# Attention with relative positions on one core: six heads of sixteen by a product over all distances instead of four, softmax sums by columns of ones, an update on GpSimd

## The reference, cut to what matters

```
x = _layernorm(src, ln1_g, ln1_b)
q, k, v = (x @ wq), (x @ wk), (x @ wv)            # 16 heads of 8
pos = arange(S - 1, -S, -1)                       # all distances
p = (concat([sin(pos * w), cos(pos * w)]) @ wp)   # (2S - 1, 16, 8)
ac = einsum('bihd,bjhd->bhij', q, k)
bd_full = einsum('bihd,phd->bhip', q, p)
bd = bd_full[:, :, i, i - j + S - 1]              # shift by the row
att = softmax((ac + bd) * scale, axis=-1)
src = src + einsum('bhij,bjhd->bihd', att, v) @ wo
x2 = _layernorm(src, ln2_g, ln2_b)
sel = sigmoid(x2 @ sel_w); scores, idx = top_k(sel, 4)
...                                               # experts, src + moe_out
x = x + 0.5 * L1_ffn(layernorm(x))
```

## Time and profile before

| | |
|---|---|
| median of 3 runs | 2732.15 us |
| the profiled execution's own time | 2728.11 us |
| its span, first to last instruction | 2726.4 us |
| PE busy, share of the span | 2436.3 us, 89% |
| DVE busy | 1929.8 us, 71% |
| ACT busy | 1581.3 us, 58% |
| POOL busy | 1557.1 us, 57% |
| mean granted clock of PE | 0.963 |

### The profile page before, as it was taken

The page is one execution under the profiler, slowest core; times in us unless marked ns, Lnnn a source line. Parts: engine busy times, 40 slices in busy tenths (PEclk is TensorE's granted clock), DMA queues, the critical chain, the costliest instruction groups (busy, mean ns, idle before and its releaser), DMA issues. The chain is left out here.

```text
span 2726.4 us, 59982 instructions
## 1 busy us (share of the span) xinstructions
PE 2436.3 (89%) x19038; PEld 1835.0 (67%) x19038; DVE 1929.8 (71%) x5169; ACT 1581.3 (58%) x4641; POOL 1557.1 (57%) x2343
## 2 busy tenths in 40 slices
PE   7999799799977999999988988999799999998898
PEld 5788677578865777777777335665577777777733
DVE  4554388455546899999876456776589999987645
ACT  2332244333326999999930226777699999993022
POOL 4322666332324678888743655554567888874365
PEclk9999899899998999999999997999899999999999
DMA  3720366370005455555455126553445545445512
GB/s 121 311 82 1 74 141 141 120 301 1 1 22 137 124 137 140 137 136 137 130 186 151 46 62 143 114 111 82 105 130 136 137 135 142 137 127 178 158 53 64
DMA packets 302396, 326.64 MB, mean 120 GB/s; under 512 B 31718, under 2 KB 274150, under 8 KB 294902
## 3 DMA queue, kind: packets, MB, share of 16 engines
q1 hardware_dynamic: 252934, 280.83, 37.9%
q0 software_dynamic: 12288, 25.19, 3.3%
q10 hardware_dynamic: 36864, 16.79, 2.1%
HBM read 133.36 MB, written 185.01 MB: 117 GB/s over the span
## 5 line engine op out<-in xcount | busy, mean ns | idle before, releaser
L2073 DVE TENSOR_REDUCE a_nm<-a_sr 128x2 f32<-128x512 f32 x256 | 166.9, 685 | 69.2 <-PE a_sr L1805 68.2
L3207 POOL TENSOR_TENSOR f4o_kv<-a5b_room 128x256 f32<-128x256 f32 x192 | 140.2, 731 | 107.7 <-DVE a5b_room L3075 102.6
L3207 POOL TENSOR_TENSOR f6o_kv<-a5b_room 128x256 f32<-128x256 f32 x192 | 140.3, 731 | 97.6 <-DVE a5b_room L3075 91.8
L2978 ACT ACTIVATE f6a_pr<-f6a_sr,f6a_nm 128x256 f32<-128x256 f32 x384 | 181.4, 486 | 12.0 <-DVE f6a_nm L3063 10.9
L2978 ACT ACTIVATE f4a_pr<-f4a_sr,f4a_nm 128x256 f32<-128x256 f32 x384 | 181.4, 486 | 9.5 <-DVE f4a_nm L3063 7.8
L3075 DVE TENSOR_TENSOR a5b_room<-f4a_ur,f4a_turn 128x512 f32<-128x512 f32 x192 | 131.2, 684 | 44.1 <-PE f4a_ur L2815 43.7
L2837 PE MATMUL f6a_sr<-all_ks,all_qs 96*128 96x256 bf16 x512 | 144.0, 281 | 13.6 <-ACT f6a_pr L2978 10.1
L2837 PE MATMUL f4a_sr<-all_ks,all_qs 96*128 96x256 bf16 x512 | 143.7, 281 | 13.8 <-ACT f4a_pr L2978 10.4
L3075 DVE TENSOR_TENSOR a5b_room<-f6a_ur,f6l_turn 128x512 f32<-128x512 f32 x192 | 131.5, 685 | 34.4 <-PE f6a_ur L2815 33.9
L2854 PE MATMUL f6a_tr<-all_table,f6a_pr 128*128 128x128 f32 x1024 | 154.8, 274 | 0.0
L2854 PE MATMUL f4a_tr<-all_table,f4a_pr 128*128 128x128 f32 x1024 | 154.7, 273 | 0.0
(11 more groups left out here) (672 smaller groups left out, 8481.8 us busy)
## 6 DMA issues: line engine op xcount, KB each, us to landing
slots<-f_zero SPq DMA_DIRECT2D x100, 512.0 KB, 6.1
f4a_slide<-f4o_kv SPq DMA_DIRECT2D x64, 383.0 KB
f6a_slide<-f6o_kv SPq DMA_DIRECT2D x64, 383.0 KB
f4o_kv<-f4a_slide SPq DMA_DIRECT2D x64, 256.0 KB
f6o_kv<-f6a_slide SPq DMA_DIRECT2D x64, 256.0 KB
f4o_src<-slots SPq DMA_DIRECT2D x128, 64.0 KB, 2.2
slots<-f4m_y ACTq DMA_DIRECT2D x128, 64.0 KB, 2.3
f6o_src<-slots SPq DMA_DIRECT2D x128, 64.0 KB, 2.2
```

The lines of the kernel that those rows point to most:

```text
L2073: nc.vector.tensor_reduce(nm[:, r // 2, t, at_:at_ + 2], sr[:, g % SB, :].rearrange("p (x s) -> p x s", x=2), AX.X, ALU.max, negate=True). ...
L2978: last = nc.scalar.activation(pr[:, n % 4, x, :], from_, ACT.Exp, bias=nm[:, n % SB, x:x + 1], scale=sign, accum_out=zs[:, b[1], t, h:h + 1])
L3207: nc.gpsimd.tensor_tensor(rr[:, o % RAW, :], tmp[:, o % 2, 0, :], tmp[:, o % 2, 1, :], ALU.add)\
```

## The change

Six parts, all in the attention of f4 and f6, and none elsewhere:

1. Heads 1, 3, 5, 9, 11 and 13 slide, instead of 1, 5, 9, 13. The table of distances in SBUF now holds heads that are not evenly spaced, so it is filled by 18 DMAs instead of 3 (once, in f4).
2. The softmax sums no longer come from ACT's accumulator. The value matrix gets columns of ones beside each pair of heads, set once, so that the product with the values also gives the sums; `y` uses 512 columns of its bank instead of 256.
3. At the end of a batch ACT copies `y` (512 columns), PE transposes it (four blocks), DVE takes reciprocals of the sums and multiplies, PE transposes back (two blocks), ACT copies, then `wo` follows.
4. x gets its half of the result by two POOL instructions in slot 15 instead of one DVE instruction in slot 9.
5. The small work stands in other slots.
6. SP's order has six shifts in a step: 9, 11, 13, then 1, 3, the write, then 5.

```
-SLID = H // QUAD
+SLIDING = (1, 3, 5, 9, 11, 13)
+SLID = len(SLIDING)
...
-            rows = bass.AP(part.tensor, part.offset + QUAD * OFFSETS, [[P * OFFSETS, run], [H * OFFSETS, HD], [1, SLID * OFFSETS]])
-            sp.dma_start(self.ms[first * HD:(first + run) * HD, :, :].rearrange("s a m -> s (a m)"), rows).then_inc(self.stacked, 16)
+            for n, hs in enumerate(SLIDING):
+                rows = bass.AP(part.tensor, part.offset + head_at(hs) * OFFSETS, [[P * OFFSETS, run], [H * OFFSETS, HD], [1, OFFSETS]])
+                sp.dma_start(self.ms[first * HD:(first + run) * HD, n, :], rows).then_inc(self.stacked, 16)
...
+        for first in (16, 2 * C):
+            nc.vector.memset(bass.AP(whole.tensor, whole.offset + first, [list(whole.ap[0]), [QUAD * C, 2 * TT], [C + 1, 2],
+                                                                         [QUAD * HD, QUAD]]), 1.0).then_inc(self.vm_zero, 1)
...
-        AT = {"xt": 8, "qk": 10, "x2t": 12, "sel": 14, "src": 11, "ln": 3}
+        AT = {"y": 4, "yt": 5, "yb": 7, "xt": 8, "o": 9, "qk": 10, "x2t": 14, "sel": 15, "src": 11, "ln": 3}
...
-                shift(s - 2, 9)
-                shift(s - 2, 13)
-                shift(s - 1, 1)
+                for hs in SLIDING:
+                    if hs >= AHEAD:
+                        shift(s - 2, hs)
+                for hs in SLIDING:
+                    if hs < LATEST:
+                        shift(s - 1, hs)
                 if (2 if led else 0) <= s < B:
                     lead.write(sp, s)
                 if s == 0 and not led:
                     far.stack(sp)
-                shift(s - 1, 5)
+                for hs in SLIDING:
+                    if LATEST <= hs < AHEAD:
+                        shift(s - 1, hs)
...
-                    last = nc.scalar.activation(pr[:, n % 4, x, :], from_, ACT.Exp, bias=nm[:, n % SB, x:x + 1], scale=sign,
-                                                accum_out=zs[:, b[1], t, h:h + 1])
+                    last = nc.scalar.activation(pr[:, n % 4, x, :], from_, ACT.Exp, bias=nm[:, n % SB, x:x + 1], scale=sign)
...
-                    if n == 1:
-                        dve.wait_ge(sr.emptied, sr.done(e, NR - 1))
-                        nc.vector.reciprocal(rz[:, :, :], zs[:, par, :, :]).then_inc(rz_ready, 1)
-                        dve.wait_ge(rz_ready, i + 1)
-                        nc.vector.tensor_copy(rz8[:, :, :, :], rz[:, :, :].unsqueeze(3).to_broadcast([P, TT, H, HD]))\
-                            .then_inc(rz8_ready, 1)
+                    if n == AT["yt"]:
+                        dve.wait_ge(desk.filled, desk.nth(it, "yt"))
+                        bank = desk.bank(it, "yt").rearrange("p (h g c) -> p h g c", h=2, c=QUAD * HD)
+                        for hf in range(2):
+                            last = nc.vector.reciprocal(rz[:, hf, :, :], bank[:, hf, :, 16 * (1 - hf):16 * (1 - hf) + 2])
+                        last.then_inc(rz_ready, 1)
...
+                                rz[:, hf, :, :].unsqueeze(3).to_broadcast([P, 2 * QUAD, 2, HD]), ALU.mult)
+                        last.then_inc(yq_ready, 1)
...
-                    if n == 9:
-                        nc.vector.scalar_tensor_tensor(x_b[:, i, :, :], s1[:, :, :], 0.5, x_b[:, i, :, :],
-                                                       ALU.mult, ALU.add)
...
+                if e and n == 15:
+                    pool.wait_ge(opening.s1_aggr, e[0] + 1)
+                    if e[0]:
+                        pool.wait_ge(x_moved, e[0])
+                    nc.gpsimd.tensor_scalar(half[:, :, :], s1[:, :, :], 0.5, None, ALU.mult).then_inc(halved, 1)
+                    pool.wait_ge(halved, e[0] + 1)
+                    nc.gpsimd.tensor_tensor(x_b[:, e[0], :, :], x_b[:, e[0], :, :], half[:, :, :], ALU.add).then_inc(x_moved, 1)
```

133 lines of the change are left out of this document (76 added, 57 removed).

## The result

The changed kernel takes 2771.33 us (median of 4 runs, 2770.73 to 2780.07) where the kernel before takes 2732.62 (2728.84 to 2735.44). The ratio is 1.015, with a 95% interval of 1.0126 to 1.0174 (the two medians alone give 1.014). The forecast was 2695 us, so even the sign was wrong, and the time lies outside the range of 2662 to 2728. The profiled execution of after took 2780.07 us, 9 above its median, at a span of 2778.3.

A forecast was written before the change was run, and what follows sets the result against it. ACT, PE and DVE, each 90 to 94% busy, set the pace by passing small delays round. Terms: -60 + 5.3 + 7.6 + 5 + 5 = -37 us, giving 2691 against the profiled 2728.1, or 2695 as median; range 2662 to 2728.

The forecast's parts named there:

- The loads: Busy us per batch: DVE 30.7 to 29.1, ACT 31.8 to 29.2, PE 31.5 to 30.8, POOL 26.0 to 24.5.
- The pace: Batches of f4 and f6 shorten from 33.95 to 32.0 us; about 31 gain in full, -60 us.
- Slot 6: Head 13's band copy needs head 9's buffer, free after 7.7 us against 8.0: +0.15 us a batch, +5 us.
- Rival 3: Bands' round trips take over in slot 6, holding 3.1 us a batch: 2786 us, chance 0.09.
- The stage's end: Uncovered finish grows 2.8 us and the update on POOL 1.0 at both stage ends: +7.6 us.
- The starts: 15 more issues ahead of f4's first q and k, +5.3 us; one more shift at both stage starts, +5 us.
- Rival 4: Update on POOL blocks DVE (`gate_sum`, slot 0) up to 0.7 us a batch: 2717 us, chance 0.06.
- Rival 1: ACT was the pace and more of its load goes than counted: pace 31.0 us, 2664 us, chance 0.20.
- Rival 2: PE holds the pace by its busy time, 33.25 us a batch: 2733 us, chance 0.10.

The follow-up runs named there:

- run 9: Changed kernel with the next q and k read after head 9's band and the whole update of x back on VectorE, slot 11: 2713.61 us, ratio 0.993.
- run 4: Changed kernel with four sliding heads (1, 5, 9, 13) instead of six: 2755.21 us, ratio 1.0086.
- run 5: Run 4 with the whole update of x on VectorE again, slot 11: 2747.70 us, ratio 1.0063.
- run 7: Run 6 with the other two-input small work also moved to slots where GpSimd adds nothing: 2715.38 us, ratio 0.9945.
- run 10: Run 7 with one of three TensorE products of the positional term left out in the plain heads: 2698.75 us, ratio 0.9877.
- run 2: Changed kernel with SyncE reading the next batch's q and k after head 9's band, not ahead of it: 2737.71 us, ratio 1.0025.
- run 1: Changed kernel with only the last batch's update of x in each attention stage made by VectorE: 2761.68 us, ratio 1.0115.
- run 3: Changed kernel with the edits of run 1 and run 2 together: 2720.96 us, ratio 0.996.
- run 8: Run 7 with the tables of distances stacked by 9 DMAs instead of 18: 2717.80 us, ratio 0.9946.
- run 6: Run 3 with the gate's equality moved from slot 13 back to slot 12: 2716.22 us, ratio 0.9944.

## Why the prediction was wrong

**The loads: right.** In the stretch of the earlier trace rows, at 34.07 us a batch, DVE is busy 29.2 us a batch (forecast 29.1), ACT 29.4 (29.2), PE 31.0 (30.8), POOL 24.2 (24.5). Part of the agreement is luck: the equality's 1.05 us more in 12 batches was not in the sum.

**The pace: failed, for a part without a cause shown.** It added each engine's idle time of before to its new load and took a value near the middle, 32.0 for 33.95 us: 1.95 less. On one footing, the mean of the fifteen periods in f4 and f6, run 9, where the hold of slot 6 and the drain no longer count, has 33.24 and 33.12 us against 34.15 and 34.36 before: 0.9 and 1.2 less. In the steady batches alone the median fell from 34.45 to 32.8, 1.65 less, so more of the shortfall stands in the batches that come out longer than that.

The method failed too. It makes idle time a constant of the engine, and it is not. With ScalarE's readouts gone the period was no shorter with four heads (runs 4 and 5, where the longer equality gave VectorE load back), of VectorE's last 1.3 us nothing (run 7), of 2.4 us on TensorE 0.76 (run 10). My reading is that the batch is a sum of sixteen slots, each as long as its fullest engine, and that load taken out of an engine counts only in slots where it is the full one. The runs fit that for most slots and do not prove it: slot 3 took back 0.37 of the 0.49 us that slot 2 lost (run 7), and slot 9 grew by 0.20 where work had gone (run 10), so a slot also hangs on its neighbours. The table of slots could have been read from the trace of before.

**Slot 6: the right place, mis-sized.** This is the largest step that failed. The term was 0.15 us a batch, ends 0 and 0.7, +5 us in all. VectorE idled 26.4 us on it in 15 batches of f4, 1.8 each, and 31.4 us in f6, and taking it away gave 33.6 us (run 2), in which the lowered clock has a share that no run tells apart. The sum put 0.6 us between the start of head 9's copy and its way out, the length of VectorE's half alone. It takes 2.58: ScalarE's half starts 1.24 us later, and two issues of reads stand in front. The trace of before has the same stretch, 2.0 us, from this copy to the way out at 1083.59:

```profile
1081.59 0.54 DVE L3084 COPY f4o_kv<-f4a_ur 128x383 f32<-128x383 f32 x1
```

With it the need would have been 9.1 us against four slots of 8.0, so a hold of 1.1 us a batch, 29 us more than in the sum, and a forecast gain of 8 us instead of 37. The landing also grew, to 7.7 us, with the DMA share at 0.61.

**Rival 3: the larger of the two mechanisms that decided the sign,** given 0.09. It was to decide from 1.35 us a batch on, and the hold is 1.8. Alone it did not: without the hold the kernel is still 0.25% slower than before (run 2), without the drain 1.15% (run 1), without both 0.4% faster (run 3). The 2786 us had a hold of 3.1 us behind it; by the rival's own sum 1.8 give some 2745 us, and the drain and the pace that was not there make up the way to 2771.

**The stage's end: a term left out.** The finish grew by 2.2 us (forecast 2.8), the update by 1.6 in place of 0.42, near enough. The drain of GpSimd behind its last instruction is the second step that failed, a term that was not in the sum: 16.8 us for both stages (runs 3 and 2) where the sum had 2. Its sign stood in the earlier trace rows, an idle of 17.45 us with GpSimd's queue itself as releaser.

**The starts: right for f4, low otherwise.** The first exponentials of f4 come 5.6 us later behind the first matmul (forecast 5.3), and run 8 gives 0.37 us an issue (0.353). In f6 nothing moves ahead of the first batch, but its first two periods are 5.7 us longer, those of f4 6.5, for 2.5 expected; most of it goes with the late read (12.2 us for both stages come down to 1.9), so it is the same hold.

**Rival 4** was right in kind, not in place: no long `gate_sum` (253 ns), but the equality at 1463, held up by GpSimd's additions that were there before, since it was moved beside them. The order of the slots gave a hint: in the changed kernel slot 13 relates a plain head, slot 12 a sliding one. It does not settle it alone, since head 3, of slot 12, is a plain one before; there the equality, at 1105.64, ran between two additions of GpSimd, one that ended at 1105.33 and one that began at 1106.81. **Rival 1** is excluded by the periods of runs 4 and 5. **Rival 2**, PE by its busy time at 33.25 us, fits some slots and is wrong as a whole, since run 9 is below it: 32.64 us, read as in the earlier trace rows. It comes near there: TensorE is busy 190.9 of the 200 us from 1100 on, VectorE 187.3, ScalarE 182.7. The Trainium skill, "Perfetto Trace Analysis", section Identifying the Most-Contended Engine, calls matmul busy share a poor measure of room; here PE's busy share fell from 0.93 to 0.91 and told nothing of where it was full.

Run by run the miss of 76.3 us is: the read's place 33.6, the drain 16.8, the update's place 7.4 (run 3 to 9), and 18.5 that no run gave back. That is the pace: for pace, stage starts and slot 6 together the sum had -50 us, and the fifteen periods of f4 and of f6 in run 9 are together 32 us shorter than before. The 7.4 are read between two chips, so it is 7 or 8.

## What to carry to other kernels

Before a saving is credited to the pace, cut the steady batch into its slots and ask in each which engine has no gap; load taken from another engine there is the first to be worth nothing. Look at the mean of the periods beside the median, and at the granted clock of the long ones. When a buffer ring of two serves more users, follow the transfer that frees it through its queue, with what stands in front of it: here one read's place in a queue was worth 1.2%. And before work is given to an idle engine at a stage's end, look at what its queue does behind its last instruction.

## What the hardware did that I had not expected

- GpSimd's drain at the end of the attention block lasts 8.69 and 8.68 us in after, 8.71 in run 1, 9.3 in run 5 and 10.68 and 10.36 before. Of the 36 drains of GpSimd in the trace of after, four last over 1 us: these two and those of the two mixtures (11.2 and 11.1 us), and these four blocks are the only ones in which GpSimd issues indirect DMAs. In after the last one of f4's attention is issued at 1393.9, 16.7 us ahead of the drain. What the drain waits for stays open; no run took these DMAs away.
- TensorE's granted clock fell to half in the middle of a stage behind single waits of 1.9 to 3.2 us. Not behind each: two waits of 2.4 and 2.6 us in f6, in its fifth and eleventh batch, were followed by no fall, and these batches took 34.9 and 35.3 us.
- The time of one VectorE instruction with two inputs in SBUF ranges with its neighbours on GpSimd: the equality on 128x256 takes 416 ns in the kernel before, 489 and 519 in runs 7 and 6, 1182 in run 9, 1463 in after, 1977 in run 4 and 2190 in run 5, the 32-column sum of masks 204 in run 7 and 984 in run 6, the update 505 in run 9 and 1109 before.
- ScalarE's 32 accumulator readouts of 0.218 us a batch are 7 us of its rows, yet its busy time fell by 2.4 us a batch with the other edits on it, and the period with four heads by nothing.
